# A decoder kernel's second part: the next unit's causal attention as its own chain on two PSUM banks, the first inversion on VectorE, no constant products

## The reference, cut to what matters

```
L0: cosine attention over features | cross attention, 16 heads | int8 SiLU feed-forward
L1: ternary-weight attention       | cross attention with mixed heads | blockwise int4 feed-forward
```

```
L2a  causal linear attention: q, k = elu(xW)+1; out = sum_{s<=t} (q_t.k_s) v_s / (sum + 1e-6)
L2x  cross attention, 16 heads of 64, over latents and context
L2f  base linear + 2 of 8 low-rank experts
L3a  chunkwise delta rule (chunks of 32, 4 heads; needs T = inv(I - A) of a strictly
     lower 32 x 32 block), FIR filters of 3, 15 and 64 taps, a softmax gate over 5 paths,
     out = norm(sum_c gate_c * path_c) Wo
L3x  cross attention with rotary positions, 16 heads of 8
L3f  shared expert + 2 of 8 experts with SiLU
```

## Time and profile before

| | us |
|---|---|
| runs: 1477.33, 1478.28, 1466.74; median | 1477.33 |
| the profiled execution's own time | 1478.8 |
| its span, first to last instruction | 1476.9 |
| mean granted TensorE clock | 0.956 of full |

### The profile page before, as it was taken

One profiled execution on the slowest core, in us unless ns is written; L12 is line 12 of the kernel. 1 busy time (PEld: TensorE's weight loads), 2 busy tenths in 40 slices (PEclk: granted clock), 3 DMA queues, 4 the chain that ended last, 5 costly groups with the idle time before them and its releaser, 6 DMA issues.

```text
span 1476.9 us, 42456 instructions
## 1 busy us (share of the span) xinstructions
PE 1353.8 (92%) x18664; PEld 1189.8 (81%) x18664; DVE 1049.8 (71%) x2983; ACT 625.6 (42%) x1269; POOL 132.5 (9%) x275
## 2 busy tenths in 40 slices
PE   3799998999895899999979999989999988999986
PEld 3698887888742699898869989878989877998975
DVE  5966799668679577566777665677866578765666
ACT  4344663446468445324325433334533333542321
POOL 3111112111010000000000000100000000010000
PEclk9999999999897899989989998999999799999999
DMA  4000000000121100000000000000000000000001
GB/s 153 2 2 2 3 2 1 2 2 3 72 117 36 74 1 1 2 3 2 2 1 1 2 3 3 2 2 1 1 3 3 2 2 1 2 1 3 3 2 30
DMA packets 6520, 20.29 MB, mean 14 GB/s; under 512 B 2240, under 2 KB 4288, under 8 KB 5696
## 3 DMA queue, kind: packets, MB, share of 16 engines
q1 hardware_dynamic: 6336, 17.58, 3.3%
HBM read 16.53 MB, written 1.05 MB: 12 GB/s over the span
## 4 chain that ended last, share of the span: by engine, by line
PE 48%; DVE 12%; ACT 3%; POOL 1%; issue 1%; DVEq 0%
PE PS L2075 7%; PE PS L2214 6%; PE PS L1787 4%; PE PS L1821 4%; PE PS L1800 4%; PE PS L1832 4%; PE PS L2085 3%; DVE X L2592 2%; PE PS L1812 2%; PE PS L510 2%; PE PS L603 1%; PE PS L2524 1%; PE PS L2181 1%; DVE AR L2585 1%; POOL SC L502 1%
## 5 line engine op out<-in xcount | busy, mean ns | idle before, releaser
L2075 PEld LDWEIGHTS PS<-AR 64*64 64x64 f32 x3072 | 112.4, 144 | 6.1 <-issue 2.3
L2075 PE MATMUL PS<-AR 64*64 64x32 f32 (+1 forms) x3072 | 116.0, 227 | 0.2
L2214 PE MATMUL PS<-AR,PA 64*64 64x256 f32 (+45 forms) x2624 | 114.8, 303 | 1.2 <-ACT AR L2302 0.9
L499 POOL TENSOR_SCALAR SC<-mv 128x2 f32<-128x2 f32 x72 | 15.4, 214 | 999.4 <-DVE mv L487 998.8
L510 PE MATMUL PS<-CC 128*128 128x128 f32 x628 | 97.5, 300 | 0.0
L2214 PEld LDWEIGHTS PS<-AR,PA 64*64 64x64 f32 x2624 | 90.1, 135 | 7.4 <-issue 2.9
L510 PEld LDWEIGHTS PS<-CC 128*128 128x128 f32 x628 | 87.8, 211 | 2.9 <-issue 0.7
L1787 PE MATMUL PS<-kvt,WC 128*128 128x128 f32 x512 | 67.9, 278 | 2.6 <-ACT kvt L1839 2.0
L1800 PE MATMUL PS<-kvt,AR 128*128 128x128 f32 x512 | 68.0, 277 | 0.9 <-ACT AR L1845 0.8
L1821 PE MATMUL PS<-WC,AR 128*128 128x128 f32 x512 | 67.7, 276 | 0.4 <-ACT AR L1859 0.4
L1832 PE MATMUL PS<-AR 128*128 128x256 f32 x256 | 66.2, 385 | 0.6 <-ACT AR L1856 0.5
(11 more groups left out here) (537 smaller groups left out, 3342.3 us busy)
## 6 DMA issues: line engine op xcount, KB each, us to landing
WC<-in_cw SPq DMA_DIRECT2D x1, 5438.5 KB, 16.7
PA<-in_fd SPq DMA_DIRECT2D x1, 2624.0 KB, 9.3
PA<-in_stat SPq DMA_DIRECT2D x2, 1280.0 KB, 12.6
CC<-in_const SPq DMA_DIRECT2D x1, 1065.0 KB, 8.1
out<-X SPq DMA_DIRECT2D x1, 1024.0 KB, 6.1
PA<-in_aw SPq DMA_DIRECT2D x1, 975.0 KB, 11.5
AR<-in_raw SPq DMA_DIRECT2D x1, 832.0 KB, 8.2
AR<-in_intw SPq DMA_DIRECT2D x1, 576.0 KB, 9.1
```

The costliest lines, as they stand in the source:

```text
L2075: m = T.matmul(ps[rows, bank, n * width:(n + 1) * width], lhsT=lhs[rows, n, :], rhs=rhs(rows, n), start=True, stop=True)
L2214: m = T.matmul(out_[:, :, first:SEQ], lhsT=FD[rows, tap:tap + 64], rhs=d.vp[rows, :, first + 1 - shift:SEQ + 1 - shift], start=starts, sto ...
```

## The change

It has four parts, all in the second part of the kernel.

1. L2a is taken out of the main chain. Each stream gets a third chain, `heads`, that runs L2a of unit i while the main chain is at unit i - 1. It has banks 2 and 3, the arena from column 4096, small tiles of its own there, and writes them only after L3a of the unit before has ended (`free`, the mark `L3a.x`). Its scores go to the two banks in two pairs. POOL sets its value tile anew in each unit (three memsets).
2. L3x and L3f keep to banks 0 and 1. L3x uses the two-bank scores of the other attentions (`tensor_pairs`) and rotates the keys ahead of the norm. L3f goes through four groups of two experts, which alternate between the banks.
3. In L3a, the first step of the inverse is made on VectorE: the mask `low1` takes the other triangle, the two halves are added and scaled. The mixture of the paths is summed by VectorE with two reductions.
4. `FILL_C` is empty. All four order lists are new; on TensorE, chains 4 and 5 are now the heads, on POOL chains 2 and 3.

The diff, cut to its core:

```diff
-    for m in (1, 2, 4, 8, 16):
+    for m in (2, 4, 8, 16):
+    c["low1"] = (i64 // 2 == j64 // 2) & (i64 % 2 == 1) & (j64 % 2 == 0)
...
+        heads = [Stream(stream_sems[s], s, known, twin=st) for s, st in enumerate(streams)]
+        for hd, st in zip(heads, streams):
+            hd.s, hd.ps, hd.ar, hd.sc = st.s, PS[st.s][:, 2:4, :], st.ar[:, 4096:8256], SC[:, st.s, 480:608]
+            hd.xn, hd.on = (hd.ar[:, o:o + ST].rearrange("p (j d) -> p j d", j=TS) for o in (3072, 2048))
+            hd.xt, hd.ot = hd.ar[:, 3328:3584], hd.ar[:, 2304:2560]
...
-            V.wait_ge(*(v.at("L2x.x1") if k == "L2f" else v.now()))
+            V.wait_ge(*(v.at("L2x.x1") if k == "L2f" else v.at("L2a.x") if k == "L2x" else v.now()))
...
             V.wait_ge(*st.pool.at(f"{k}.rstd"))
+            if free:
+                V.wait_ge(*free)
...
+        def free(st):
+            return st.dve.at("L3a.x", st.before) if st.before else None
... (tensor_l2_attention)
+            for pair in ((0, 1), (2, 3)):
+                if pair[0]:
+                    yield
+                    T.wait_ge(*st.dve.at(f"{k}.masked1"))
+                for q in range(SQ):
+                    for r in pair:
+                        rows = slice(32 * r, 32 * r + 32)
+                        m = T.matmul(ps[:, r % 2, q * P:(q + 1) * P], lhsT=dst[rows, 1, q, :, :], rhs=dst[rows, 0, q, :, :],
+                                     start=True, stop=True)
... (pool_l2_attention)
+            G.memset(st.vo[:, :, :, :, :], 0.0).then_inc(*g.up())
+            for c in range(2):
+                G.wait_ge(*g.now())
+                G.memset(st.vo[64 * c:64 * c + 64, :, c, :, HD], 1.0).then_inc(*g.up(f"{k}.vo" if c else None))
... (tensor_l3_attention)
-            T.wait_ge(*v.at(f"{k}.pairs"))
-            products(f"{k}.up0", 2, d.up[0], lambda rows, n: cc("ident32")[rows, :])
...
-            for j in range(TS):
-                T.wait_ge(*v.at(f"{k}.parts{j}"))
-                for c in range(5):
-                    m = T.matmul(d.mixed[:, j * P:(j + 1) * P], lhsT=ident, rhs=d.pr[:, o:o + P], start=(c == 0),
-                                 stop=(c == 4))
... (vector_l3_attention)
-            V.wait_ge(*p.at(f"{k}.up0"))
-            V.tensor_tensor(d.pc, d.bank[2], dd8, ALU.mult).then_inc(*v.up())
+            V.tensor_tensor(d.pc, d.up[0][:, :, 0:32], d.up[0][:, :, 32:64], ALU.add).then_inc(*v.up())
+            V.tensor_tensor(d.pc, d.pc, dd8, ALU.mult).then_inc(*v.up())
...
+            for j in range(TS):
+                V.tensor_reduce(d.mixed[:, j * P:(j + 1) * P], d.pr[:, 640 * j:640 * j + 640].rearrange(
+                    "p (c n) -> p n c", c=5), AX, ALU.add).then_inc(*v.up(f"{k}.mixed" if j else None))
... (L3f)
+        class Experts:
+            def __init__(self, st, g):
+                b = (g + 1) % 2
+                self.bank = st.ps[:, b, :]
+                self.he, self.th = st.ar[:, 512 + 512 * b:1024 + 512 * b], st.ar[:, 1536 + 512 * b:2048 + 512 * b]
+                self.out = self.bank.rearrange("p (j e d) -> p j e d", j=TS, e=2)
...
+            for g in range(NGROUP):
+                out_(g)
+                yield
+                if g + 2 < NGROUP:
+                    hidden(g + 2)
+                    yield
...
+        def tensor_head_c(hd):
+            for i in range(NITER):
+                next_head(hd, i)
+                yield from tensor_l2_attention(hd)
...
         def tensor_part_c(st):
             for i in range(NITER):
                 begin(st, "c", i)
-                yield from tensor_l2_attention(st)
                 yield from tensor_l2_cross(st)
                 yield from tensor_l2_ffn(st)
                 yield from tensor_l3_attention(st)
-                yield from tensor_rope_attention(st, "L3x", wc, st.ct)
+                yield from tensor_rope(st, "L3x", wc, st.ct)
                 yield from tensor_l3_ffn(st)
...
-        FILL_C = ("022110000000000000000000000003300000000000010000331551111101122222220022244400000000000003000000"
+        FILL_C = ("")
```

More of the change, by code:

```diff
@@ L136, in also, with at @@
         self.made[self.stream.round, name] = self.n
[L138 to L139 removed]
+    def at(self, name, round=None):
+        return self.sem, self.known[(*self.label, (round or self.stream.round, name))] if self.known else 1
     def now(self):
@@ new lines, in scalar_rope, with values @@
+        def scalar_rope(st, k, w):
+            def values():
+                scalar_values(st, k, 1)
+                yield
+            yield from scalar_norm(st, k, early=(values,))
+            rq = turning(st)
+            A.wait_ge(*st.dve.at(f"{k}.rotated"))
+            for n, (dst, mask) in enumerate(zip(operands(st), ("parity", "pair"))):
+                A.activation(dst[:, :, 1, :], rq[:, 0, n, :].rearrange("p (q t) -> p q t", q=SQ), ACT.Copy,
+                             scale=cc(mask)[:, 1:2]).then_inc(*st.act.up(f"{k}.operands" if n else None))
+            yield
+            yield from scalar_pairs(st, k, w, st.ar[:, 2048:4096])
@@ L2812, in decoder @@
             fill = [tensor_fill(FILL_C)] if engine == "tensor" else []
-            chains = [part(st) for st in streams] + [aside(sd) for sd in asides if aside] + fill
-            take_turns(chains, TURNS_C[engine])
+            chains = [part(st) for st in streams] + [aside(sd) for sd in asides if aside] + [head(hd) for hd in heads]
+            take_turns(chains + fill, TURNS_C[engine])
         all_done()
```

407 lines of the change are left out of this document (172 added, 235 removed), and 159 rows, old and new, of the table TURNS_C.

## The result

The changed kernel takes 1520.1 us (median of 4 runs, 1504.7 to 1523.2) against 1477.8 for the kernel before on the same chip: a ratio of 1.0266, 95% interval 1.0235 to 1.0297. The medians differ by 42 us. The forecast was 1417, faster: wrong in sign, and the result lies outside the range. Every median in this document is over fast executions, which leaves out one execution of e10 and one of e14.

What follows compares the result with a forecast made beforehand. The second part was taken as bound by TensorE's work plus latencies, its boundaries by latency. From 1478.8 us, -49.5 - 6 - 7 - 3 + 0 + 5 = -60.5 gave 1418.3, less 1.5: 1417; range 1376 to 1465.

Steps and rivals of the forecast that it cites:

- no constant products: Second part: removing TensorE's filler products shortens the chain outside the boundaries by 6 us, bounds 0 and 25.
- two banks: L3x and L3f on two banks: L3x longer, L3f shorter, together 0, bounds -12 and +12 us.
- heads: Three unit boundaries: L2a runs beside L3x and L3f, gaining 3 x (21.5 - 5) = 49.5 us.
- the clock: Boundaries without filling: useful share rises to 92%, near the present 90%; 5 us added, bounds 0 and 100.
- rival 4: Boundaries and last tail run at half rate without constant products, making the kernel slower: 1517 us; chance 0.05.
- Wrong: stream times from L3x to L2x still above 65 us: Sign against the forecast, which expected L2x to start about 50 us after L3x in each stream.
- last tail unchanged: Sign for the forecast: the last tail, where no L2a follows, keeps its length.
- dense stretches 2 us shorter each: Sign for the forecast: stretches from last L2x start to next L3x start shorten by 2 us each, without constant products.
- First inversion on VectorE: Dense stretches: 256 TensorE records go, gaining 7 us, bounds 0 and 9.6.
- Mixture on VectorE: L3a's mixture: two VectorE reductions replace 160 TensorE records, gaining 3 us, bounds -3 and 20.
- Rival 3: Head instructions block ready main ones in the queues, or bank waits cost the gain: about 1472 us; chance 0.08.
- Rivals 1 and 2: Boundaries limited by VectorE, 1451 us, chance 0.14; or rounds falling to TensorE's useful work, 1374 us, chance 0.10.

Runs made afterwards that it cites:

- e10: The changed kernel with the mixture's sum put back on TensorE, no constant products added; 1520.0 us.
- e14: The kernel before without second-part constant products, with first inversion and mixture on VectorE and score products two strips at a time; 1556.3 us.
- e1: The kernel before with the 259 constant products of its second part taken out, nothing else; 1521.7 us.
- e6: The kernel before without second-part constant products and with first inversion and mixture on VectorE; 1520.7 us.
- e5: The kernel before, constant products kept, with first inversion and mixture on VectorE; 1487.7 us.
- e13: The kernel before with only the score products of L3x and L2a reordered to two strips at a time, still in four banks; 1490.4 us.
- e8: The changed kernel with 132 constant products where its trace shows TensorE idle for 0.9 us or more; 1501.5 us.
- e7: The kernel before, constant products kept, with only the first inversion on VectorE; 1462.7 us.

## Why the prediction was wrong

The result by steps that were measured one on top of the other, in us:

| step | from | to | forecast | measured |
|---|---|---|---|---|
| no constant products | before | e1 | -6 | +44 |
| first inversion and mixture on VectorE | e1 | e6 | -10 | -1 |
| two strips at a time | e6 | e14 | (in "two banks": 0) | +36 |
| heads, order, L3f in two banks | e14 | changed | -49.5 | -36 |
| the clock | | | +5 | (in each of the above) |
| sum | | | -60.5 | +42 |

The steps depend on each other through the clock, so another order of steps gives other numbers: the sums on VectorE are +10 with the constant products kept (e5) and -1 without, the constant products +44 ahead of the sums and +33 behind them (e5 to e6), the strips +12 (e13) and +36.

*No constant products: the step that failed first.* The forecast priced 80 us of useless work by how much of it is on the path, and set its effect on the clock apart, at +5. It had the right rule and its price in rival 4 and gave it a chance of 0.05, because of two falls of the clock in the trace of before, one in spite of constant products and one without a gap. That was reading the exceptions: the row to read was the clock of 1.00 over two boundaries in which useful work filled only 76%. 259 products held the clock there, and the trace of before could not show what is there without them: e1 has 0.87 and 0.83 in the same boundaries. The Trainium skill ("TensorE: Matmul & The Clock Gate", section "Why this matters for your kernels") states the rule against idle gaps, and e1 agrees with it: 44 us. Idle gaps don't explain the second kind of place: the fall at 1224.4 us comes after 8 us without any.

*The point of decision of rival 4 was right.* "Under about 0.8 over these stretches": boundary 1 shows 0.95, the other two and the tail 0.73 to 0.75. Its price, 1517, came within 3 us of the result, but by luck in good part. It took a full gain of 60 off 100 us lost on short bursts in the boundaries; the strips aren't in it, and neither are the 25 us by which the dense stretches grew.

*L3x on two banks: the step that failed second.* The forecast counted VectorE's and ScalarE's extra latency in the two-bank form and set TensorE's side to nothing, with bounds of 12 either way. The trace of before had the price: four-strip passes in this part, two-strip passes of the same product in the first. In four banks (e13, e14) it is 28 us of TensorE's time, 12 of the kernel's with the clock held and 36 without.

*Heads: the overlap was right, the stream times were not.* L2a leaves the main chain and runs beside L3x, and from e14 to the changed kernel that is worth 36 us of 49.5, of which 177 - 152 = 25 are time at the half rate that is gone. But the sum took L3x and L3f as they were, and they grew. "Wrong: stream times from L3x to L2x still above 65 us" is met by four of six, 70.7 to 85.6 us; boundaries 2 and 3 take 108.7 and 83.5 us, not 75 to 80; "last tail unchanged" is +20 us, "dense stretches 2 us shorter each" is 2, 9 and 14 longer. Where the clock held, the boundary did better than forecast: 73.1 us in boundary 1 and 66.3 in boundary 3 of e8, for 78.

*First inversion on VectorE: sign right, too small.* 15 us (e7) for 7. The forecast took busy time as its bound, 9.6; the gain goes over it because the lost time falls with it, from 65 to 50 us by the median. Why the clock holds in its dense stretches wasn't measured by itself.

*Mixture on VectorE: the doubt on record was the case.* "At twice the time the pair costs 3.3 and the gain is gone": the reductions take 1.24 us each, a pair 2.4, 1.5 times the estimate, and with the constant products kept it costs 25 us. The estimate was made from reductions that read along a row; this one reads with a stride of 128 elements and writes 128 results a row instead of 8, and which of the two costs isn't shown. The 3 us a unit of TensorE's work that go are replaced by waits of up to 5 us, 7.9 in e5.

*Rival 3, the order doesn't deliver,* fell in its first half: the heads overlap. Its second half, that the bank waits cost what is gained, was not run by itself. *Rivals 1 and 2,* both faster, fell: VectorE shows 70.3 of 108.7 us in boundary 2 and 54.4 of 83.5 in boundary 3, far from full.

What stays open: why the clock falls at 1224 us, and is at half from 940 to 960, while TensorE is busy. Products of few rows (32 of 128) and few columns (18) fill these stretches. e8 has the same half rate from 940 to 960 us although gaps were filled elsewhere, and e14 shows that more such work at two strips goes with a lower clock; that little work in the array is what lowers it is an inference. No run had such a stretch with only the size of its products changed. Also open is what made the dense stretches longer.

No version of the changed order was found that beats the kernel before: the nearest is e8, 1501.5. e7, the old order with one of the change's edits, beats both, by 0.9% and 3.8%.

## What to carry to other kernels

Useless work that keeps a clock up is load-bearing: before it is removed, look for the stretches where the clock is high although useful work leaves gaps, and price them at half rate; if products are to fill, place them in the gaps of the trace of that very kernel. Compare kernels stage by stage, cut at the same events, and check by its tiles which stage an instruction belongs to before a distance is read from it. When a stage is squeezed into fewer PSUM banks, price TensorE first: here two strips at a time on two banks took TensorE twice the time of four on four. And measure edits one on top of the other: here the same edit was worth 12 us or 36, by whether the clock was held.

## What the runs showed of the hardware that was not expected

- A filler need not be large: 32 of 128 columns of weights held the clock as well as 128 in the old order (0.961 and 0.956), and its weights loaded in 116 ns instead of 210.
- A record of a product of 32 rows starts every 29 ns with four strips in turn and every 59 with two, at full clock. In four banks, but two strips for four sequences and then the other two (e13), it is 47 ns: so most of the loss is the order and not the number of banks.
- A reduction on VectorE over a stride of 128 elements, 640 elements to 128, takes 1.24 us, where 512 contiguous ones to 8 take 0.684: 1.9 ns an element against 1.3.
- TensorE can be busy without a gap and be at 1.2 GHz throughout (1224.4 to 1251.7 us), after 8 us at full rate that were busy without a gap too.
- Executions of one kernel differ in the granted clock, and the time follows it: the kernel before, 1467 us at 0.965 and 1483 at 0.953.
